# A two-layer tower on one core: turns of tiles moved between a layer's head, its attention loop and the feed-forward part of the layer before

## The chip, the core and the metric

The kernel runs on 1 core of one Trainium2 chip. Times are microseconds of the device. The time before is 2112.12 us, the median of 3 runs (2109.9 to 2117.12). Engines are called as the profile calls them: PE is TensorE's matrix multiply (PEld its weight load), DVE VectorE, ACT ScalarE, POOL GpSimd, SP the engine that issues the DMAs (SPq its queue).

## What is computed

8 x 256 tokens of width 192. First a token embedding with a layer norm, then four layers with banded attention (12 heads of 16; a token sees those within 64 positions), each with a feed-forward part of width 768; then an attention over channels, a feed-forward part with 4 experts, an unbanded attention, and one with 8 experts. The four layers in the reference:

```python
for l in range(L):
    q = heads(h @ Wq[l] + bq[l])
    k = heads(h @ Wk[l] + bk[l])
    v = heads(h @ Wv[l] + bv[l])
    a = band_attention(q, k, v, mask)
    a = a.transpose(0, 2, 1, 3).reshape(B, S, Hd)
    h = layer_norm(h + a @ Wo[l] + bo[l], ln1_s[l], ln1_b[l])
    f = jax.nn.gelu(h @ W1[l] + b1[l], approximate=False)
    h = layer_norm(h + f @ W2[l] + b2[l], ln2_s[l], ln2_b[l])
...
h = h + _L1_attn_ref(_layernorm(h, axis=-1), ...)      # softmax(q k^T * SCALE) v, 12 heads
```

## The kernel before

The 2048 tokens are 16 tiles of 128 (NT), in 4 groups of 4 (GT). Each engine's program is written out by hand in order; engines meet at semaphores, and an engine does nothing that stands behind a wait. A hardware loop (Fori) runs the four layers.

**Turning a tile.** To multiply h it must lie with its features on the partitions. TensorE transposes a tile in two halves into a PSUM bank (L364, in pe_transpose), ScalarE copies it, rounded, to xx (L569, act_split), and VectorE makes the two remainders from the same bank (L654, L655, dve_split). Turns use banks 0 and 1 by turns (BX), so the turn of tile t waits, through xx_ready, for the split of tile t - 2.

**A layer's head.** At its start TensorE turns tiles 0 to 3, then makes the projections of group 0 (items 0 to 6: three of q and k, L382 to L386, and four of v, L392 to L396) and the first three of group 1 (AHEAD), with the turns of tiles 4 to 15 between them (beside). q and k are cut into three bf16 pieces each: ScalarE copies the projection (L587, L589), VectorE makes the pieces of group 0 (L663 to L665, dve_pieces), GpSimd those of later groups (L894 to L897, pool_pieces) and those of v (L931 to L934, pool_v). SP writes the pieces to DRAM (L908) and reads them back by heads (L917) into qx and kx, once all three pieces of the group are there. ScalarE's third copy of group 1 (act_qk with n = 5) waits for the first pieces that GpSimd makes of group 1, since it writes the same qf buffer; it stands ahead of the first exponential in ScalarE's program. GpSimd makes v pieces first (pool_v of group 0, then pool_pieces of group 1).

**The attention loop** runs over 96 pairs of heads p (PAIRS; 12 pairs to one sequence of 256 tokens). At pair p TensorE does, in this order, the scores of p (L469 adds the mask, L472; allowed two pairs ahead of the exponentials), the values of p - 5 (L501 to L503), the transposes of the probabilities of p - 3 (L483), and at pairs 1, 4, 7, 10 one more projection of group 1 into bank 3 (BM[0]); later groups have theirs at every third pair. ScalarE does the exponentials (L604, numbers 2p and 2p + 1) and between them the copy of the turned probabilities of p - 3 (L615). VectorE does max of p (L682), the remainder lo of p - 4 (L688), then at the pair behind a v projection its copy to vf (L674), then a step of finishing a tile (L702 to L715).

**Behind the loop** the attention's output of a group is turned (turn k = 1, from xn), multiplied by Wo (L392 to L396), added (L753, residual, half 0), normed (statistics L762 and L766, GpSimd's scale L843 and L844, affine L796 to L805), and turned again (k = 2, from h). The feed-forward part is pe_hidden: 24 steps n (6 to a group) with the features of n (L382 to L386, into banks 2 and 3), ScalarE's Gelu (L643) and the second product of n - 2 (L562 x8, into banks 4 to 7; the first of a group waits until the residual, half 1, has read the group before). under() hangs turns ahead of steps: k = 2 of group g + 1 at step 6g + 2, k = 1 of group g + 2 at 6g + 3, and the product with Wo at 6g + 5. A step without a turn takes 2.45 us. On VectorE dve_tail gives the order; for g = 0 to 4 it does the first affine of group g + 1, residual and statistics (half 1) of g - 1, the turns' splits (2, g + 1), the second affine of g - 1, and then the turn, residual and statistics of g + 2. GpSimd's pool_tail follows with the scales and with hb, the next residual's summand (L850).

## Time and profile before

| | before |
|---|---|
| median of 3 runs | 2112.12 us (2109.9 to 2117.12) |
| the profiled execution | 2105.01 us, its span 2103.2 us |
| PE busy | 1575.0 us, 75% of the span |
| DVE busy | 1356.9 us, 65% |
| ACT busy | 1109.5 us, 53% |
| POOL busy | 717.1 us, 34% |
| granted TensorE clock, mean | 0.876 of full |
| chain that ended last | PE 48%, DVE 24%, issue 12%, ACT 6%, DMA 4%, POOL 3% |

The span goes by stages: a banded attention takes 156 us (93 to 249, then from 393 to 549 and so on), what lies between two of them some 144 us, of which the feed-forward steps are the larger part; the four layers end at about 1275 us, the unbanded attention's loop runs from 1617 to 1784. Shares over the whole span say little here, since each stage has another engine that is late; the views by stretch and by time say more. In them a line has its start in us from the span's start, how long it (or the run of equal ones, x4 and so on) took, and in brackets how long the engine had been idle and what ended that. The granted clock is a share of 2.4 GHz; its two levels are 1.2 and 2.4 GHz.

### The profile page before, as it was taken

To read this page: it belongs to the slowest core of one execution; us is meant where nothing else is said; L and a number is where in the kernel's file an instruction comes from. 1 tells how busy PE (TensorE), PEld (TensorE's weight loads), DVE (VectorE), ACT (ScalarE), POOL (GpSimd) and SP (SyncE) were. 2 spreads that over 40 slices of the span, in tenths; PEclk is the share of its full clock that TensorE was granted. 3 is DMA by queue.
4 is the path that set the end of the run, shared out by engine and by line. 5 is a ranking of instruction groups with operands and counts; after the bars stand their busy time and mean duration, and the time that the engine had idled before them with its cause. 6 is when DMAs were issued, how large, how long until landed. Compare 5 with 4: busy or idle time off the path is not lost.

```text
span 2103.2 us, 47757 instructions
## 1 busy us (share of the span) xinstructions
PE 1575.0 (75%) x14634; PEld 1320.4 (63%) x14634; DVE 1356.9 (65%) x3622; ACT 1109.5 (53%) x3351; POOL 717.1 (34%) x989
## 2 busy tenths in 40 slices
PE   0588777798787798786898783875945887649993
PEld 0477666576576676675676672754944666449993
DVE  4688865688765789665888655243436998544444
ACT  0499632698523799323898221323524997225651
POOL 5644123534122542133541231012544340025551
PEclk9999889899798899798999795877976999669996
DMA  5868000875000955003864000004746580137875
GB/s 133 167 111 101 16 1 2 152 96 83 1 1 25 155 80 72 1 2 52 136 96 49 1 1 12 1 21 143 239 126 91 83 100 2 40 120 239 242 233 167
DMA packets 191388, 178.63 MB, mean 85 GB/s; under 512 B 23056, under 2 KB 176208, under 8 KB 190992
## 3 DMA queue, kind: packets, MB, share of 16 engines
q1 hardware_dynamic: 183824, 158.19, 38.4%
q0 software_dynamic: 7296, 17.18, 2.5%
q8 instruction: 130, 2.13, 0.5%
q14 instruction: 138, 1.13, 0.2%
HBM read 132.96 MB, written 42.34 MB: 83 GB/s over the span
## 4 chain that ended last, share of the span: by engine, by line
PE 48%; DVE 24%; issue 12%; ACT 6%; DMA 4%; POOL 3%; SPq 1%; DVEq 1%; ACTq 0%; POOLq 0%
DVE ptl L688 7%; PE bank L1261 6%; PE bank L483 5%; PE bank L562 4%; ACT pth L615 3%; PE bank L501 2%; PE bank L364 2%; DVE neg_max L682 2%; ACT prob L604 2%; PE bank L1247 2%; PE bank L382 2%; DVE h L805 2%; DMA kx<-qk_rows 1%; PE bank L472 1%; PE bank L386 1%
## 5 line engine op out<-in xcount | busy, mean ns | idle before, releaser
L604 ACT ACTIVATE prob<-bank,neg_max 128x192 f32<-128x192 f32 (+1 forms) x960 | 417.1, 440 | 67.5 <-DVE neg_max L682 32.2
L688 DVE TENSOR_TENSOR ptl<-bank,pth 128x512 f16<-128x512 f32 x480 | 329.3, 686 | 34.7 <-ACT pth L615 26.6
L682 DVE TENSOR_REDUCE neg_max<-bank 128x2 f32<-128x384 f32 (+1 forms) x480 | 273.6, 570 | 92.9 <-PE bank L472 90.3
L483 PE MATMUL bank<-ident,prob 128*128 128x128 f32 x1920 | 310.0, 285 | 0.0
L615 ACT ACTIVATE pth<-bank 128x512 f16<-128x512 f32 x480 | 286.9, 598 | 6.4 <-PE bank L483 6.4
L569 ACT ACTIVATE xx<-bank 128x256 fp32r<-128x256 f32 x256 | 94.2, 384 | 365.8 <-PE bank L364 360.0
L501 PE MATMUL bank<-v,pth 128*128 128x32 bf16 x1920 | 199.4, 180 | 107.1 <-DVE ptl L688 94.0
L501 PEld LDWEIGHTS bank<-v,pth 128*128 128x128 f16 x1920 | 154.0, 96 | 197.6 <-DVE ptl L688 187.4
L483 PEld LDWEIGHTS bank<-ident,prob 128*128 128x128 f32 x1920 | 205.6, 143 | 0.2
L604 ACT ACTIVATION_READ_ACCUMULATOR prob<-bank,neg_max 128x1 f32 x960 | 202.6, 211 | 0.0
L503 PE MATMUL bank<-v,ptl 128*128 128x32 bf16 x1920 | 193.6, 176 | 0.0
L502 PE MATMUL bank<-v,pth 128*128 128x16 bf16 x1920 | 190.1, 169 | 0.0
L843 POOL TENSOR_SCALAR rstd<-mv 128x4 f32<-128x4 f32 x52 | 12.0, 231 | 491.0 <-DVE mv L766 485.0
L472 PE MATMUL bank<-kx,qx 96*128 96x192 bf16 (+1 forms) x960 | 169.9, 259 | 7.5 <-DMA kx<-qk_rows 5.3
L364 PE MATMUL bank<-ident,h 128*128 128x128 f32 x256 | 58.6, 352 | 141.2 <-DVE xx L655 88.7
L502 PEld LDWEIGHTS bank<-v,pth 128*128 128x128 f16 x1920 | 157.0, 97 | 0.2
L503 PEld LDWEIGHTS bank<-v,ptl 128*128 128x128 f16 x1920 | 154.7, 96 | 0.0
L643 ACT ACTIVATE fbuf<-bank,b 128x512 f32<-128x512 f32 x96 | 65.9, 687 | 164.7 <-PE bank L386 164.7
L364 PE MATMUL bank<-ident,xn 128*128 128x128 f32 x256 | 62.2, 372 | 117.5 <-DVE xx L655 63.1
L469 PE MATMUL bank<-mask,ident 128*128 128x384 bf16 x384 | 130.4, 340 | 23.6 <-DMA kx<-qk_rows 23.6
L562 PE MATMUL bank<-w,fbuf 128*128 128x192 f32 x768 | 143.0, 332 | 0.0
L562 PEld LDWEIGHTS bank<-w,fbuf 128*128 128x128 f32 x768 | 133.7, 195 | 8.3
(273 smaller groups left out, 4250.0 us busy)
## 6 DMA issues: line engine op xcount, KB each, us to landing
xn<-in_e_seg SPq DMA_DIRECT2D x34, 768.0 KB, 6.8
qx<-qk_rows SPq DMA_DIRECT2D x240, 96.0 KB, 5.0
kx<-qk_rows SPq DMA_DIRECT2D x240, 96.0 KB, 7.2
qk_rows<-fbuf SPq DMA_DIRECT2D x80, 192.0 KB, 2.8
w<-in_e_w SPq DMA_DIRECT2D x23, 576.0 KB, 4.6
qk_rows<-piece_c SPq DMA_DIRECT2D x40, 192.0 KB, 3.0
hb<-in_e_w SPq DMA_DIRECT2D x11, 576.0 KB, 4.3
y_rows<-mask SPq DMA_DIRECT2D x8, 768.0 KB, 8.7
```

The source lines that it names most:

```text
L364: last = nc.tensor.transpose(bank[BX[t % 2]][:, c * P:c * P + P], src[:, t, c * P:c * P + P], ident[:, :])
L469: nc.tensor.matmul(o, ident_bf, mask[:, 2 * b + qt, :].unsqueeze(1).to_broadcast([P, 2, D]), start=True, stop=False)
L472: last = nc.tensor.matmul(o[:, e, :], qx[0:ROWS, b % 3, hd + e, qt * P:qt * P + P], kx[0:ROWS, b % 3, hd + e, ks], start=not banded, stop= ...
L483: last = nc.tensor.transpose(bank[BT[p % 2]][:, (2 * e + c) * P:(2 * e + c) * P + P], prob[:, qt, hd % PROBS, c * P:c * P + P], ident[:, :])
L501: nc.tensor.matmul(o2, pth[:, p % 3, w], v[:, 0:32], start=(c == 0), stop=False)
L502: nc.tensor.matmul(o1, pth[:, p % 3, w], v[:, 32:48], start=False, stop=False)
L503: last = nc.tensor.matmul(o2, ptl[:, p % 2, w], v[:, 0:32], start=False, stop=(c == 1))
L562: last = nc.tensor.matmul(bank[BY[t]][:, 0:D], fbuf[:, (n - 2) % 4, t * P:t * P + P], w2[:, c, :], start=(c == 0), stop=(c == FC - 1))
L604: nc.scalar.activation(prob[:, qt, hd % PROBS, c0:c0 + n], scores_at(u // 2, n)[:, u % 2, :], ACT.Exp, bias=neg_max[:, tile_no % 3, hd:hd ...
L615: nc.scalar.activation(pth[:, p % 3, :], bank[BT[p % 2]][:, :], ACT.Copy).then_inc(hi_ready.sem, 1)
L682: nc.vector.tensor_reduce(neg_max[:, t % 3, hd:hd + 2], scores_at(p, D if banded else S), AX.X, ALU.max, negate=True).then_inc(max_ready.s ...
L688: nc.vector.tensor_tensor(ptl[:, p % 2, :], bank[BT[p % 2]][:, :], pth[:, p % 3, :], ALU.subtract)\
```

## The change

1. **Tiles 0 to 3 of the next layer** are turned in the feed-forward part, ahead of steps 20 and 21 (under, with first), and split by VectorE at the end of dve_tail's round g = 3, behind the second affine of group 2. For the first layer they are turned ahead of the loop.
2. **The last group's statistics, scale and affine** leave dve_tail. VectorE does them in the next layer's head: the statistics behind the third pieces, the affine behind the last v copy of group 0. GpSimd's scale and hb of that group stand at the start of the next round of the loop, the scale ahead of pool_v of group 0, hb behind it.
3. **Tiles 8 to 15** are no longer turned in the head, but in the attention loop, one each at pairs 2, 3, 5, 6, 8, 9, 11 and 12 (next_turn), in bank 3, behind that pair's other work. The turn of a tile waits for the split of the tile before, or for the copy of the v projection before; a projection at pairs 4, 7, 10 waits for the split of the tile before. The unbanded attention does the same.
4. **In dve_tail** the splits (2, g + 1) come directly behind the first affine, ahead of residual and statistics, and the splits (1, g + 2) ahead of the second affine.
5. **SP** reads the first sequence's q and k by fours of heads, as soon as each piece is written (12 reads for each of three), and TensorE's scores wait for each four.

The core of the diff:

```diff
-        def pe_transpose(pe, it, s, t, src, ready, turn, n):
+        def pe_transpose(pe, it, s, t, src, ready, turn, n, inside=False):
 
             pe.wait_ge(ready.sem, ready.at(turn, n))
-            pe.wait_ge(xx_ready.sem, xx_ready.at(it, s - 1))
+            pe.wait_ge(xx_ready.sem, xx_ready.at(it, s if inside else s - 1))
+            o = bank[BM[0] if inside else BX[t % 2]]
             for c in range(2):
             last.then_inc(xt_done.sem, 1)
...
-            steps = {2 + i: (lambda i=i: (tile(GT + 2 * i), tile(GT + 2 * i + 1))) for i in range((NT - GT) // 2)}
-            steps["xx"] = xx
+            steps = {2: lambda: (tile(GT), tile(GT + 1)), 3: lambda: (tile(GT + 2), tile(GT + 3))}
+            steps["xx"], steps["inside"] = xx, lambda t: tile(t, True)
             return steps
 
-        def under(turn, out=None):
+        def next_turn(p):
+
+            if 2 <= p < 2 + 12 and p % 3 != 1:
+                return 2 * GT + 2 * (p // 3) - (p % 3 == 0)
+            return None
+        def under(turn, first, out=None):
+            for i in range(2):
+                steps[FC * (NG - 1) + 2 + i] = lambda i=i: (first(2 * i), first(2 * i + 1))
             return steps
...
         def pe_scores(pe, it, p, banded):
             b, qt, hd = where(2 * p)
+            if b == 0 and hd % 4 == 0 and qt == 0:
+                pe.wait_ge(first_in[hd // 4].sem, first_in[hd // 4].at(it, 16 * 12))
+            elif b and p % (PAIRS // B) == 0:
...
         def pe_attention(pe, it, banded, w, before):
 
             for n in range(ITEMS + AHEAD):
+                if n == 1:
+                    pe.wait_ge(y_read.sem, y_read.at(it, 0))
                 if n == ITEMS:
                     pe.wait_ge(xx_ready.sem, xx_ready.at(*before["xx"](2 * GT)))
                 pe_qkv(pe, it, n // ITEMS, n % ITEMS, w)
                 if n in before:
                     before[n]()
-            pe.wait_ge(xx_ready.sem, xx_ready.at(*before["xx"](NT)))
                     pe_turn_probs(pe, it, p - 3)
                 if next_projection(p):
                     g, i = next_projection(p)
+                    if i == 0:
+                        pe.wait_ge(xx_ready.sem, xx_ready.at(*before["xx"](NT)))
+                    elif p and next_turn(p - 1):
+                        pe.wait_ge(xx_ready.sem, xx_ready.at(*before["xx"](next_turn(p - 1) + 1)))
                     pe_qkv(pe, it, g, i, w)
+                if next_turn(p):
+                    if next_projection(p - 1):
+                        g, i = next_projection(p - 1)
+                        pe.wait_ge(vf_ready.sem, vf_ready.at(it, 4 * g + i - 3 + 1))
+                    before["inside"](next_turn(p))
...
             act.wait_ge(xt_done.sem, xt_done.at(it, s + 1))
             nc.scalar.activation(xx[:, 0:2, t * P:t * P + P],
-                                 bank[BX[t % 2]][:, 0:2 * P].rearrange("p (a n) -> p a n", a=2),
+                                 bank[BM[0] if inside else BX[t % 2]][:, 0:2 * P].rearrange("p (a n) -> p a n", a=2),
...
+                if next_turn(p):
+                    split["inside"](next_turn(p))
...
                     dve_pieces(dve, ch, it, n)
                 elif n < ITEMS:
                     dve_v(dve, it, 0, n - 3, banded)
+                if n == 2 and banded:
+                    dve_last_stats(dve, ch, it)
                 if n in split:
                     split[n]()
+                if n == ITEMS - 1 and banded:
+                    dve_affine(dve, ch, it, 0, NG - 1, 1)
...
                     if i >= 3:
                         dve_v(dve, it, g, i - 3, banded)
+                if p and next_turn(p - 1):
+                    split["inside"](next_turn(p - 1))
...
+        def dve_last_stats(dve, ch, it):
+
+            dve_stats(dve, ch, it, 1, NG - 1, y_read, NT)
...
             def out(g):
-                dve_turn(dve, it, 1, g)
                 dve_residual(dve, ch, it, 0, g)
                 dve_stats(dve, ch, it, 0, g, o_read)
 
+            dve_turn(dve, it, 1, 0)
             out(0)
             dve_turn(dve, it, 1, 1)
             dve_affine(dve, ch, it, first(0), 0, 0)
-            dve_residual(dve, ch, it, 0, 1)
-            dve_stats(dve, ch, it, 0, 1, o_read)
+            out(1)
             dve_turn(dve, it, 2, 0)
             for g in range(NG + 1):
                 if g + 1 < NG:
                     dve_affine(dve, ch, it, first(g + 1), g + 1, 0)
+                    dve_turn(dve, it, 2, g + 1)
                 if g:
                     dve_residual(dve, ch, it, 1, g - 1)
+                if 1 <= g < NG:
                     dve_stats(dve, ch, it, 1, g - 1, y_read)
-                if g + 1 < NG:
-                    dve_turn(dve, it, 2, g + 1)
-                if g:
+                if g + 2 < NG:
+                    dve_turn(dve, it, 1, g + 2)
+                if 1 <= g < NG:
                     dve_affine(dve, ch, it, second(g - 1), g - 1, 1)
                 if g + 2 < NG:
                     out(g + 2)
+                if g == NG - 1:
+                    for t in range(GT):
+                        dve_split(dve, it + 1, t, t)
 
...
+                if g == 1:
+                    pool.wait_ge(first_out[i].sem, first_out[i].at(it, 32))
+                else:
+                    pool.wait_ge(pieces_out.sem, pieces_out.at(it, 96 * (g - 1)))
...
-            for i in range(3):
-                if g == 0:
+            def write(i, done):
...
-            sp.wait_ge(pieces_out.sem, pieces_out.at(it, 96 * (g + 1)))
...
+            if g == 0:
+                for i in range(4):
+                    if i < 3:
+                        sp.wait_ge(first_pieces.sem, first_pieces.at(it, i + 1))
+                        write(i, first_out[i])
+                    if i:
+                        sp.wait_ge(first_out[i - 1].sem, first_out[i - 1].at(it, 32))
+                        read(0, slice(4 * (i - 1), 4 * i), first_in[i - 1])
+                read(1, slice(0, HEADS), qk_in[1])
+            else:
+                for i in range(3):
+                    sp.wait_ge(next_pieces.sem, next_pieces.at(it, 3 * (g - 1) + i + 1))
+                    write(i, pieces_out)
+                sp.wait_ge(pieces_out.sem, pieces_out.at(it, 96 * g))
+                for b in (2 * g, 2 * g + 1):
+                    read(b, slice(0, HEADS), qk_in[b % 3])
...
-            for g in range(NG + 1):
-                if g < NG:
+            for g in range(NG):
+                if g < NG - 1:
                     pool_rstd(pool, ch, 0, g + 1 - NG, g, 1e-12)
...
             with pool.Fori(0, L) as it:
                 ch.enter(it, 160)
+                pool_rstd(pool, ch, it, 0, NG - 1, 1e-12)
                 pool_v(pool, ch, it, 0)
+                pool_hb(pool, it, normed(2, NT - GT) - 2 * NT, NG - 1, row_bo)
                 pool_pieces(pool, ch, it, 1)
                 pool_v(pool, ch, it, 1)
...
+            pool_rstd(pool, ch, L, 0, NG - 1, 1e-12)
+            pool_hb(pool, L, normed(2, NT - GT) - 2 * NT, NG - 1, row_bo)
...
+            for t in range(GT):
+                act_split(act, 0, t, t)
             with act.Fori(0, L) as it:
-                for t in range(GT):
-                    act_split(act, it, t, t)
-                act_attention(act, it, True, beside(lambda t: act_split(act, it, t, t)))
+                act_attention(act, it, True, beside(lambda t, inside=False: act_split(act, it, t, t, inside)))
...
-            for g in range(NG + 1):
-                if g < NG:
+            for g in range(NG):
+                if g < NG - 1:
                     dve_stats(dve, ch, 0, 0, g, None)
                 if g:
                     dve_affine(dve, ch, 0, g - NG, g - 1, 1)
+            for t in range(GT):
+                dve_split(dve, 0, t, t)
             with dve.Fori(0, L) as it:
                 ch.enter(it, 512)
-                for t in range(GT):
-                    dve_split(dve, it, t, t)
-                dve_attention(dve, ch, it, True, beside(lambda t: dve_split(dve, it, t, t)))
+                dve_attention(dve, ch, it, True, beside(lambda t, inside=False: dve_split(dve, it, t, t, inside)))
...
+            dve_last_stats(dve, ch, L)
+            dve_affine(dve, ch, L, 0, NG - 1, 1)
...
+            def first_turn(it, t, inside=False):
+                pe_transpose(pe, it, t, t, h, h_ready, it, normed(2, t) - 2 * NT, inside)
+
+            for t in range(GT):
+                first_turn(0, t)
                 pe.wait_ge(wa_ready.sem, wa_ready.at(it, 1))
                 pe.wait_ge(xx_ready.sem, xx_ready.at(it, GT))
-                pe_attention(pe, it, True, wa, beside(first_turn, lambda n: (it, n)))
...
                 pe_hidden(pe, it, wb, w2[0], tok_hidden,
                           under(lambda k, g: pe_turn(pe, it, k, g, 12 if (k, g) == (2, 2) else
                                                      16 if (k, g) == (2, 3) else None),
+                                lambda t: first_turn(it + 1, t),
                                 lambda g: pe_out_group(pe, it, wb, g)))
```

## Rows read from the trace of the kernel before

**Rows 1.** Stretches: length; PE, PEld, DVE, ACT, POOL busy us (instructions); granted clock, DMA share, GB/s.

```profile
93.00:249.00 156.00, 135.94 (x1918) 109.02 (x1916) 135.36 (x281) 138.10 (x504) 60.22 (x89) 0.97 0.62 94
249.00:272.00 23.00, 15.41 (x62) 11.60 (x60) 15.52 (x65) 4.51 (x12) 3.58 (x6) 0.50 0.00 1
```

**Rows 2.** TensorE in order of time, layer 0's last products: start, length, [idle before <-releaser].

```profile
351.72 4.06 PE L562 MATMUL bank<-w,fbuf 128*128 128x192 f32 x24
```

**Rows 3.** ScalarE in order of time: T, and exp 26.

```profile
392.85 0.78 ACT L587 ACTIVATE qf<-bank,bqk,q_scale 128x512 f32<-128x512 f32 x1 [5.39 <-POOL fbuf L897]
...
412.92 0.43 ACT L604 ACTIVATE prob<-bank,neg_max 128x192 f32<-128x192 f32 x1
```

**Rows 4.** GpSimd and the SP queue in order of time, feed-forward part and hand-over.

```profile
306.45 3.60 POOL L850 TENSOR_TENSOR hb<-h,row_bo 128x192 f32<-128x192 f32 x4 [2.65 <-DVE h L805]
...
358.95 1.04 POOL L844 TENSOR_TENSOR rstd<-rstd,neg_half 128x4 f32<-128x4 f32 x1 [0.18 <-POOL rstd L843]
378.40 0.34 POOL L931 CAST v<-vf 128x192 bf16<-128x192 f32 x1 [13.21 <-DVE vf L674]
...
388.75 0.61 POOL L894 CAST fbuf<-qf 128x512 bf16<-128x512 f32 x1 [0.33 <-POOL v L934]
...
380.40 2.75 SPq L917 DMA_DIRECT2D qx<-qk_rows  x6
```

**Rows 5.** VectorE in order of time, the hand-over.

```profile
355.81 1.15 DVE L753 TENSOR_TENSOR h<-bank,hb 128x192 f32<-128x192 f32 x4 [3.67 <-PE bank L562]
...
357.93 0.41 DVE L766 BATCH_NORM_AGGREGATE mv<-stats 128x2 f32<-128x6 f32 x4
...
371.51 0.69 DVE L663 TENSOR_TENSOR qf<-qf,fbuf 128x512 f32<-128x512 f32 x1 [4.07 <-ACT fbuf L589]
...
376.88 0.28 DVE L654 TENSOR_TENSOR xx<-bank,xx 128x128 fp32r<-128x128 f32 x1
```

**Rows 6.** TensorE in order of time, feed-forward parts of layers 0 and 1.

```profile
302.38 1.15 PE L364 MATMUL bank<-ident,h 128*128 128x128 f32 x4 [3.44 <-DVE xx L655]
...
306.87 0.60 PE L364 MATMUL bank<-ident,xn 128*128 128x128 f32 x4
...
343.07 0.53 PE L382 MATMUL bank<-xx,wb_hi 128*128 128x512 f32 x1
...
347.97 0.53 PE L382 MATMUL bank<-xx,wb_hi 128*128 128x512 f32 x1
...
626.40 0.60 PE L364 MATMUL bank<-ident,h 128*128 128x128 f32 x4
...
634.48 0.53 PE L382 MATMUL bank<-xx,wb_hi 128*128 128x512 f32 x1
```

**Rows 7.** VectorE in order of time, feed-forward part of layer 0.

```profile
301.78 0.29 DVE L654 TENSOR_TENSOR xx<-bank,xx 128x128 fp32r<-128x128 f32 x1
...
343.40 1.15 DVE L753 TENSOR_TENSOR h<-bank,hb 128x192 f32<-128x192 f32 x4 [10.34 <-PE bank L562]
...
351.45 0.69 DVE L805 SCALAR_TENSOR_TENSOR h<-hb,rstd,ln_b 128x128 f32<-128x128 f32 x1
```

**Rows 8.** TensorE and VectorE in the attention of layer 1, full clock.

```profile
397.69 0.41 PE L469 MATMUL bank<-mask,ident 128*128 128x384 bf16 x1
...
398.30 0.56 DVE L682 TENSOR_REDUCE neg_max<-bank 128x2 f32<-128x384 f32 x1 [0.57 <-PE bank L472]
399.11 0.69 DVE L688 TENSOR_TENSOR ptl<-bank,pth 128x512 f16<-128x512 f32 x1 [0.26 <-ACT pth L615]
```

**Rows 9.** The same engines just before, lower clock.

```profile
394.37 0.51 PE L392 MATMUL bank<-wa_hi,xx 128*128 128x192 f32 x1
...
395.54 0.54 PE L469 MATMUL bank<-mask,ident 128*128 128x384 bf16 x1
...
396.44 0.56 DVE L682 TENSOR_REDUCE neg_max<-bank 128x2 f32<-128x384 f32 x1 [1.18 <-PE bank L472]
```

**Rows 10.** The page's costliest groups: ScalarE's copy of a turned tile.

```profile
L569 ACT ACTIVATE xx<-bank 128x256 fp32r<-128x256 f32 x256 | 94.2, 384 | 365.8 <-PE bank L364 360.0
```

68 lines of the change are left out of this document (31 added, 37 removed).

## The prediction

> **What bounds the kernel now.** I read the stages first, then the hand-over between two layers, engine by engine. In the banded attention no engine has room: of 156.0 us ScalarE is busy 138.1, TensorE 135.9, VectorE 135.4 [rows 1]. So a wait put into that loop lengthens it, and work taken out of the gaps between stages shortens the kernel. The largest gap is the hand-over. TensorE ends a layer's feed-forward part at 355.78 (351.72 + 4.06) [rows 2], and the first softmax work follows the third copy of the next group's projections on ScalarE, L587, at 392.85; call that instant T. ScalarE's idle time before it, 5.39 us, was ended by GpSimd's L897, and exp number 26 (the first of pair 13) starts at 412.92, T + 20.07 [rows 3]. The hand-over is thus 37.1 us, and what ends last in it is a queue on GpSimd: v pieces from 378.40, q/k pieces of group 1 from 388.75 to T [rows 4]. The transfers of q and k land at about the same time. All times are those of the profiled execution (2105.0 us, span 2103.2); it is 7.1 us below the median of 2112.1, and I add every difference to the median.
>
> **Hand-over (three times, layers 0 to 1, 1 to 2, 2 to 3).** The last group's statistics and affine, the turns of tiles 0 to 3 and those of tiles 8 to 15 leave the path. The new path from the end of the feed-forward part: projection item 0 at the full clock 1.3 (half a plain step of 2.45 [rows 6] and its landing), two ScalarE copies of 0.78 [rows 3], three pieces on VectorE 5.4 (376.88 - 371.51), hence 8.3 [rows 5]. The residual L753 (1.15) holds item 1 for as long and is covered. Then dve_last_stats, 1.4 (from the residual's end, 356.96, to the aggregation's, 358.34) [rows 5]: 9.7. GpSimd now runs, ahead of pool_v, pool_rstd, which waits for these statistics: 1.65 to the end of L844 at 359.99 [rows 4], 11.4. pool_v takes 10.35 (378.40 to 388.75): 21.8. pool_hb of the last group, which used to run before, stands behind it: 3.6 (L850 x4): 25.4. The first q/k pieces 4.1: T at 29.6 instead of 37.1 [rows 3, 4]. **Saved: 7.5 each, 22.** VectorE's affine, under 5 long [rows 7], ends near 18 and is covered by pool_v. SP's earlier, smaller reads cost nothing as long as they land before T: written after 4.7 and 6.5, even with 36 reads issued 0.46 apart (six in 2.75 us before [rows 4]) the last lands near 32, and it is wanted by pair 4.
>
> **First layer and the unbanded attention.** In the prologue one affine and one set of statistics leave the path, about 5 (estimated from rows 5 and 7), while GpSimd gets pool_hb in its queue (3.6) and the wait for the scale (1.65): about +0.5. The unbanded attention has neither change: VectorE's first v copy stands behind the same pieces and splits as before, so GpSimd starts and ends as before: 0.
>
> **Feed-forward part (four times).** Two stalls go. At step 8 TensorE sits 3.44 us for VectorE's split of tile 8 and goes on at the lower clock; the step lasts 8.5, from 298.3 (302.38 less the gap and the first turns' 0.60) to 306.87 [rows 6]. VectorE splits at 301.78 only because residual and statistics come first [rows 7]. With the split at the end of the affine, 2.4 earlier (residual 1.15, statistics 1.4 [rows 5]), and the clock kept, the step is 5.1 long (two transposes' wait 1.6, features 1.3, values 1.2, and up to 1.0 since the second product now waits for the residual): 3.4 saved. Step 14 is its like: 634.48 - 626.40 = 8.08, to 4.8: 3.3 saved [rows 6]. One stall comes, and it is larger. The new turns of tiles 0 and 1 stand at step 20, of 2 and 3 at step 21; tile 2 needs bank 0 back, so TensorE waits for VectorE's split of tile 0. But VectorE's queue has, ahead of it, residual, statistics, the wait for GpSimd's scale and the whole affine of group 2: 343.40 to 352.1 [rows 7]. From the start of step 20 (343.07) tile 2 can go after 9.6, and step 21 then takes 4.5 cold (as from 302.38 to 306.87); before, both steps took 347.97 - 343.07 = 4.9 [rows 6]. Lost 9.2, of which some 6.7 are a gap. **Net +2.5, four times +10.** ScalarE's Gelu and everything else is queued behind TensorE there.
>
> **The loop (five times): the term that decides.** Tiles 8 to 15 are turned at pairs 2, 3, 5, 6, 8, 9, 11, 12, all through bank 3, which the projections of pairs 1, 4, 7, 10 use too. Each of these eleven pairs (2 to 12) now ends on TensorE with an item that waits for VectorE's last operation of the same pair, and the next pair's scores are queued behind that item. VectorE in turn takes max, lo and only then the split or v copy. So the engines go round in a ring: split to TensorE's start 0.6 (301.78 to 302.38) [rows 6, 7]; the turn of one tile 0.2 (at the lower clock two take 0.8 of the 1.15 at 302.38); scores to VectorE's max 0.61 (397.69 to 398.30); max 0.5, lo 0.6 (0.56 and 0.69 less what overlaps), then the next split [rows 8]. That is 2.5 a pair; with a projection (0.6) and a v copy in place of the turn and the split once in three pairs, these take about 7.65. Before, the 13 pairs up to exp 26 ran at 1.4 each [rows 3]. I start from T: projection, scores 2, v copy, turn and scores 3 bring the first split to T + 5.6, and eleven pairs on, exp 26 starts at T + 30.6: **+10.5 at the full clock.** At the lower clock a projection takes 1.17 (394.37 to 395.54), scores to max 0.90 (395.54 to 396.44), a turn 0.4: 3.0 a pair with a split and 9.5 for three; exp 26 at T + 36.5, **+16.4** [rows 9]. (Between T and the end of pair 1 TensorE has just been idle, so it starts low.) In the unbanded attention, with wider max and no mask product, the same ring gives +11 and +15.
>
> Which clock? TensorE's work, 135.9 / 96 = 1.4 us a pair, fills 56% of a ring pair of 2.5 us; at the lower clock, where a part of it doubles, about three quarters of one of 3.0 (an estimate). A stretch busy 15.41 of 23.00 us, 67%, was granted 0.50 throughout; the attention, busy 87%, 0.97 [rows 1]. So I take the lower level (1.2 GHz) for three quarters of the ring. The Trainium skill ("TensorE: Matmul & The Clock Gate", Part 1) says that the default state is throttled and that activity releases it; were two thirds busy enough for that, the ring would run at 2.4 GHz from early in each attention. The 23 us just named speak against it.
>
> **Sum.** Full clock: first layer 0.5, hand-overs -22, feed-forward +10, rings 4 x 10.5 + 11 = 53: +41. Lower clock: rings 4 x 16.4 + 15 = 81: +69. Three quarters of the way: +61, so 2166 for a profiled execution and **2173 by the median**. Removed work is nil: the same transposes, copies and splits are done, plus four tiles turned for a layer that doesn't come (in the last feed-forward part, under the stall).
>
> **Rivals.**
> A, the forecast: the ring at mostly the lower clock, 2160 to 2190. 0.5.
> B, the ring at the full clock, since the pairs' own transposes keep the grant up: 2112 + 41 = 2153. 0.25.
> C, no ring: the waits are met early, and a turn costs the loop only its ScalarE copy, 8 x 0.38 = 3.1 an attention [rows 10]: 0.5 - 22 + 10 + 15.5 = +4, 2116. Speaks for it: ScalarE is the busiest engine [rows 1]. Against: the order on TensorE and VectorE is fixed, and each link of the ring has its row. 0.1.
> D, faster: the turns ride in the loop's idle share (ScalarE idles 18 of 156 us [rows 1]) and cost nothing; what is left is 0.5 - 22 + 10 = -11.5, 2100. It decides as soon as an attention pays less than 2.3 us for its eight turns (11.5 / 5). Against: the same. 0.1.
> E, SP's 36 small reads land after T and hold pairs 2 and 4, or the delayed v pieces of group 1 hold pair 29: up to 5 us more an attention, 2190 to 2200. 0.05.
> That the layer's first tiles aren't turned early in effect is part of the sum: tiles 2 and 3 wait at step 21.
>
> **How the numbers follow.** A, B and E hold 0.8: the range is 2135 to 2195, its low end 18 below B for links that overlap more than their durations say, its high end in E. Faster by over 0.3% (6 us, about what a measurement of this kernel tells from none): 0.1, mainly D. Within: 0.1, C. Slower: 0.8.
>
> **What would show it.** Right: TensorE idle before L364 near the end of each feed-forward part for 6 to 7 us, released by VectorE's split; no 3.4 us gaps at steps 8 and 14; T 29 to 30 us after the feed-forward part's end, still released by GpSimd; in pairs 2 to 12 TensorE's idle time ended by VectorE's split, pairs 2.5 to 3.1 us apart, the granted clock near a half; exp 26 30 to 37 us after T. Wrong: if pairs stay at 1.4 to 1.7 us, the ring doesn't exist and C or D holds; if T comes below 25, GpSimd's queue isn't the bound of the new hand-over; if the gap at step 21 is missing, 37 us of the sum are gone.

## The result, and the profile of the changed kernel

The changed kernel takes **2181.1 us** (median of 4, 2178.6 to 2193.0) against 2111.0 for the kernel before (2104.7 to 2117.1): a ratio of 1.034, 95% interval 1.029 to 1.039. Its profiled execution took 2183.1 us, span 2181.1; that of before had a span of 2103.2. So 77.9 us have to be found. The prediction was 2173, range 2135 to 2195, slower.

The page of the changed kernel says where to look, though not yet why. First its busy times, then its group for VectorE's max (line, engine, operation, count | busy, mean ns | idle time before, and what ended most of it):

```profile
PE 1623.7 (74%) x14642; PEld 1354.6 (62%) x14642; DVE 1368.5 (63%) x3630; ACT 1115.8 (51%) x3356; POOL 707.7 (32%) x989
...
L707 DVE TENSOR_REDUCE neg_max<-bank 128x2 f32<-128x384 f32 (+1 forms) x480 | 273.6, 571 | 182.4 <-PE bank L485 180.2
```

And that group on the page of the kernel before:

```profile
L682 DVE TENSOR_REDUCE neg_max<-bank 128x2 f32<-128x384 f32 (+1 forms) x480 | 273.6, 570 | 92.9 <-PE bank L472 90.3
```

VectorE, ScalarE and GpSimd are about as busy as before; TensorE is busy 49 us more with eight more instructions, which fits the lower mean of its granted clock, 0.848 against 0.876. VectorE's idle time ahead of its max, ended by the scores, has doubled: 90 us more, with not a microsecond more work.

Then four landmarks in ScalarE's instructions divide every layer: the last Gelu, T, exp 26 and the last exp. In order of time, for the turn from layer 0 to layer 1, and T and exp 26 of layer 3:

```profile
379.90 0.69 ACT L668 ACTIVATE fbuf<-bank,b 128x512 f32<-128x512 f32 x1 [1.77 <-PE bank L389]
...
413.25 0.78 ACT L610 ACTIVATE qf<-bank,bqk,q_scale 128x512 f32<-128x512 f32 x1 [10.34 <-POOL fbuf L939]
...
450.90 0.42 ACT L627 ACTIVATE prob<-bank,neg_max 128x192 f32<-128x192 f32 x1 [0.85 <-DVE neg_max L707]
...
1047.85 0.78 ACT L610 ACTIVATE qf<-bank,bqk,q_scale 128x512 f32<-128x512 f32 x1 [10.21 <-POOL fbuf L939]
...
1079.31 0.42 ACT L627 ACTIVATE prob<-bank,neg_max 128x192 f32<-128x192 f32 x1 [0.54 <-DVE neg_max L707]
```

The same four instants in every kernel of this study, from its profiled execution (us; the five attentions are layers 0 to 3 and the unbanded one; each ratio is to the kernel before on the same chip, whose median was 2111.0 for the changed kernel, 2116.2 for e1 to e4, 2113.4 for e5 to e8, 2114.4 for e9 to e11):

| kernel | median | ratio, 95% | T to exp 26, five attentions | exp 26 to last exp | last exp to last Gelu, four layers | last Gelu to next T, three |
|---|---|---|---|---|---|---|
| before | 2111.0 | 1 | 20.0 20.1 20.4 20.4 20.9 | 130.6 132.0 131.0 132.0 129.3 | 109.0 110.7 110.4 110.4 | 40.9 40.8 41.1 |
| changed | 2181.1 | 1.034 (1.029-1.039) | 36.7 37.7 37.8 31.5 36.3 | 134.5 133.3 132.2 134.7 130.2 | 114.3 113.3 114.4 112.4 | 33.4 33.0 33.1 |
| e1 | 2101.9 | 0.994 (0.992-0.996) | 19.4 19.7 20.3 20.2 20.2 | 130.2 132.3 132.8 131.3 129.3 | 112.3 113.8 114.3 113.0 | 33.3 33.2 33.3 |
| e2 | 2165.5 | 1.024 (1.021-1.028) | 36.0 37.6 37.8 33.6 36.3 | 133.2 133.7 132.0 133.4 130.3 | 106.3 106.1 106.5 107.2 | 33.6 33.1 33.0 |
| e3 | 2130.4 | 1.006 (1.004-1.008) | 24.0 24.0 24.0 25.4 26.0 | 133.2 132.1 132.5 132.6 131.9 | 112.4 113.5 113.7 113.1 | 33.4 33.4 33.0 |
| e4 | 2087.4 | 0.987 (0.984-0.991) | 21.2 21.0 20.1 19.5 20.7 | 131.4 129.7 130.3 132.6 129.3 | 103.2 103.2 103.1 103.2 | 41.4 41.1 40.8 |
| e5 | 2178.4 | 1.031 (1.027-1.035) | 36.2 35.3 35.2 36.7 36.3 | 131.5 133.1 133.8 131.3 129.8 | 114.3 113.0 112.4 112.5 | 33.3 33.1 33.3 |
| e6 | 2071.8 | 0.981 (0.978-0.985) | 20.0 19.7 19.4 20.2 21.0 | 131.4 131.8 130.6 132.1 129.3 | 106.0 107.1 107.2 106.2 | 33.4 33.3 33.5 |
| e7 | 2091.1 | 0.990 (0.986-0.993) | 18.9 18.7 18.7 18.9 20.6 | 139.4 140.0 138.5 139.2 129.2 | 106.5 107.2 106.4 106.5 | 31.2 31.2 31.1 |
| e8 | 2066.5 | 0.979 (0.975-0.983) | 19.0 20.3 19.0 20.3 19.9 | 129.3 132.2 129.4 131.1 129.3 | 106.5 106.2 106.5 106.4 | 33.3 33.3 33.1 |
| e9 | 2065.8 | 0.979 (0.974-0.984) | 19.3 18.7 18.7 19.1 20.1 | 133.9 136.0 132.0 129.4 129.3 | 106.0 105.2 106.0 106.1 | 31.4 31.1 31.6 |
| e10 | 2054.3 | 0.974 (0.970-0.978) | 20.3 18.8 18.9 18.4 20.9 | 130.8 129.4 128.2 129.9 130.7 | 105.1 105.0 107.0 105.0 | 31.5 31.4 31.2 |
| e11 | 2142.5 | 1.014 (1.008-1.020) | 30.3 30.3 30.4 30.4 31.2 | 128.7 129.6 129.0 130.2 129.9 | 111.7 111.6 113.5 112.8 | 33.1 33.0 33.3 |

**Where the 77.9 us are**, by the first two rows before rounding: T to exp 26, 16.8 + 17.6 + 17.4 + 11.0 + 15.4 = **+78.2**; last exp to last Gelu **+14**; exp 26 to last exp **+9.9**; last Gelu to T **-23.4**; the first T +2.0 (it lies between 88 and 94 us in all profiled executions, so this one isn't explained by the change); the rest -2.7. The stretch from the last exp of the unbanded attention to the end, which no kernel here touches, took 334 to 345 us in these executions, so spans alone compare to a few us; the columns of the table do better.

**The pairs (answers to [rows 8, 9, 10]).** TensorE in order of time in pairs 1 to 7 of layer 1, only the instructions that waited, then four of layer 3:

```profile
414.08 0.53 PE L395 MATMUL bank<-wa_hi,xx 128*128 128x192 f32 x1 [10.23 <-ACT qf L610]
417.23 0.66 PE L367 MATMUL bank<-ident,h 128*128 128x128 f32 x2 [1.10 <-DVE vf L699]
419.63 0.69 PE L367 MATMUL bank<-ident,h 128*128 128x128 f32 x2 [0.25 <-DVE xx L680]
422.66 0.53 PE L395 MATMUL bank<-wa_hi,xx 128*128 128x192 f32 x1 [0.85 <-DVE xx L680]
426.40 0.66 PE L367 MATMUL bank<-ident,h 128*128 128x128 f32 x2 [0.44 <-DVE vf L699]
429.40 0.69 PE L367 MATMUL bank<-ident,h 128*128 128x128 f32 x2 [0.45 <-DVE xx L680]
432.43 0.53 PE L395 MATMUL bank<-wa_hi,xx 128*128 128x192 f32 x1 [0.44 <-DVE xx L680]
...
1057.12 0.36 PE L395 MATMUL bank<-wa_hi,xx 128*128 128x192 f32 x1 [1.26 <-DVE xx L680]
1059.96 0.41 PE L367 MATMUL bank<-ident,h 128*128 128x128 f32 x2 [0.92 <-DVE vf L699]
1062.40 0.44 PE L367 MATMUL bank<-ident,h 128*128 128x128 f32 x2 [0.92 <-DVE xx L680]
1064.87 0.36 PE L395 MATMUL bank<-wa_hi,xx 128*128 128x192 f32 x1 [0.92 <-DVE xx L680]
```

Every item through bank 3 waits for VectorE's last operation of the pair. Pairs with a turn are 3.00 apart in layer 1 (426.40 to 429.40) and three pairs 9.77 (422.66 to 432.43); in layer 3 they are 2.44 and 7.75. VectorE goes round with them, here in layer 1:

```profile
427.73 0.56 DVE L707 TENSOR_REDUCE neg_max<-bank 128x2 f32<-128x384 f32 x1 [1.57 <-PE bank L485]
428.21 0.68 DVE L713 TENSOR_TENSOR ptl<-bank,pth 128x512 f16<-128x512 f32 x1
428.81 0.28 DVE L679 TENSOR_TENSOR xx<-bank,xx 128x128 fp32r<-128x128 f32 x1
429.00 0.34 DVE L680 SCALAR_TENSOR_TENSOR xx<-xx,lo_rows,bank 128x128 fp32r<-128x128 f32 x1
430.76 0.56 DVE L707 TENSOR_REDUCE neg_max<-bank 128x2 f32<-128x384 f32 x1 [1.42 <-PE bank L485]
```

Split (429.34) lets the turn go at 429.40, the turn lets scores go, the scores the max at 430.76, then lo, then split. The two stretches from T to exp 26, of layers 1 and 3 (columns as in [rows 1]):

```profile
413.00:451.00 38.00, 31.17 (x223) 24.00 (x224) 17.17 (x43) 20.88 (x74) 16.81 (x28) 0.50 0.96 172
1048.00:1079.00 31.00, 20.35 (x222) 16.18 (x223) 16.77 (x42) 20.20 (x73) 15.23 (x26) 0.88 0.97 179
```

Nearly the same work, 223 and 222 TensorE instructions: at the lower level (1.2 GHz, granted 0.50) 38 us, at mostly the upper one (2.4 GHz) 31.

**The feed-forward part (answers to [rows 6, 7]).** TensorE at step 8 and at steps 20 and 21 of layer 0, then VectorE at step 21:

```profile
322.99 0.89 PE L367 MATMUL bank<-ident,h 128*128 128x128 f32 x4 [0.86 <-DVE xx L680]
...
361.22 0.60 PE L367 MATMUL bank<-ident,h 128*128 128x128 f32 x4
...
370.63 1.14 PE L367 MATMUL bank<-ident,h 128*128 128x128 f32 x4 [6.35 <-DVE xx L680]
```

```profile
361.42 1.15 DVE L784 TENSOR_TENSOR h<-bank,hb 128x192 f32<-128x192 f32 x4 [5.62 <-PE bank L585]
...
365.62 1.40 DVE L831 SCALAR_TENSOR_TENSOR hb<-h,mv,ln_s 128x192 f32<-128x192 f32 x4 [1.68 <-POOL rstd L883]
...
370.05 0.28 DVE L679 TENSOR_TENSOR xx<-bank,xx 128x128 fp32r<-128x128 f32 x1
```

The old gap of 3.44 us is 0.86. The new one is 6.35: tiles 0 and 1 are turned at 361.22, and VectorE splits tile 0 at 370.05, behind the residual and the affine of group 2.

**The hand-over (answers to [rows 4, 5]).** GpSimd in order of time; the feed-forward part's last products end at 383.76:

```profile
394.84 0.23 POOL L882 TENSOR_SCALAR rstd<-mv 128x4 f32<-128x4 f32 x1 [24.05 <-DVE mv L801]
...
396.25 0.34 POOL L986 CAST v<-vf 128x192 bf16<-128x192 f32 x1
...
407.00 2.22 POOL L889 TENSOR_TENSOR hb<-h,row_bo 128x192 f32<-128x192 f32 x4 [0.17 <-POOL v L989]
409.17 0.61 POOL L936 CAST fbuf<-qf 128x512 bf16<-128x512 f32 x1
```

T follows at 413.25, 29.5 us after that end, and the chain is the queue described in the prediction: scale, v pieces, sums, pieces.

### The profile page after: what moved, and what is told of

It reads as the page before. It is cut to its first block, busy times and chain, and to the rows that moved or that the text cites. A ratio compares the mean times of both kernels' runs of the same rounds, so it can differ in the third digit from the quotient of the medians.

```text
span 2181.1 us, 47962 instructions
## 1 busy us (share of the span) xinstructions
PE 1623.7 (74%) x14642; PEld 1354.6 (62%) x14642; DVE 1368.5 (63%) x3630; ACT 1115.8 (51%) x3356; POOL 707.7 (32%) x989
## 4 chain that ended last, share of the span: by engine, by line
PE 48%; DVE 25%; issue 13%; POOL 6%; ACT 5%; DMA 2%; DVEq 1%; SPq 1%; POOLq 0%; ACTq 0%
DVE ptl L713 7%; PE bank L1316 6%; PE bank L585 4%; PE bank L496 4%; PE bank L367 3%; PE bank L514 2%; PE bank L485 2%; ACT pth L638 2%; DVE neg_max L707 2%; DVE xx L680 2%; DVE h L840 2%; PE bank L1302 2%; PE bank L395 2%; PE bank L482 2%; PE bank L385 1%
## 5 line engine op out<-in xcount | busy, mean ns | idle before, releaser
L627 ACT ACTIVATE prob<-bank,neg_max 128x192 f32<-128x192 f32 (+1 forms) x960 | 416.3, 438 | 132.5 <-PE bank L496 69.6
L496 PE MATMUL bank<-ident,prob 128*128 128x128 f32 x1920 | 333.0, 300 | 0.0
L514 PEld LDWEIGHTS bank<-v,pth 128*128 128x128 f16 x1920 | 158.5, 98 | 177.2 <-DVE ptl L713 168.0
L496 PEld LDWEIGHTS bank<-ident,prob 128*128 128x128 f32 x1920 | 220.7, 151 | 0.2
L485 PE MATMUL bank<-kx,qx 96*128 96x192 bf16 (+1 forms) x960 | 177.2, 268 | 0.0
L367 PE MATMUL bank<-ident,h 128*128 128x128 f32 x264 | 65.3, 363 | 145.2 <-DVE xx L680 82.7
L515 PEld LDWEIGHTS bank<-v,pth 128*128 128x128 f16 x1920 | 159.9, 98 | 1.1
L367 PEld LDWEIGHTS bank<-ident,h 128*128 128x128 f32 x264 | 35.3, 174 | 172.1 <-DVE xx L680 88.2
L585 PEld LDWEIGHTS bank<-w,fbuf 128*128 128x128 f32 x768 | 132.5, 194 | 12.6 <-issue 5.2
```

The lines of the kernel that those rows point to most:

```text
L367: last = nc.tensor.transpose(o[:, c * P:c * P + P], src[:, t, c * P:c * P + P], ident[:, :])
L485: last = nc.tensor.matmul(o[:, e, :], qx[0:ROWS, b % 3, hd + e, qt * P:qt * P + P], kx[0:ROWS, b % 3, hd + e, ks], start=not banded, stop= ...
L496: last = nc.tensor.transpose(bank[BT[p % 2]][:, (2 * e + c) * P:(2 * e + c) * P + P], prob[:, qt, hd % PROBS, c * P:c * P + P], ident[:, :])
L514: nc.tensor.matmul(o2, pth[:, p % 3, w], v[:, 0:32], start=(c == 0), stop=False)
L515: nc.tensor.matmul(o1, pth[:, p % 3, w], v[:, 32:48], start=False, stop=False)
L585: last = nc.tensor.matmul(bank[BY[t]][:, 0:D], fbuf[:, (n - 2) % 4, t * P:t * P + P], w2[:, c, :], start=(c == 0), stop=(c == FC - 1))
```

## The experiments

The diffs are against the changed kernel where nothing else is said.

**e1: the turns of tiles 8 to 15 back in the head.** This separates the ring from everything else that the change does to the attention.

```
-            steps = {2: lambda: (tile(GT), tile(GT + 1)), 3: lambda: (tile(GT + 2), tile(GT + 3))}
+            steps = {n: (lambda i=i: (tile(GT + 2 * i), tile(GT + 2 * i + 1))) for i, n in enumerate((2, 3, 4, 5, 7, 8))}
...
-            if 2 <= p < 2 + 12 and p % 3 != 1:
-                return 2 * GT + 2 * (p // 3) - (p % 3 == 0)
             return None
...
+            pe.wait_ge(xx_ready.sem, xx_ready.at(*before["xx"](NT)))
             for p in range(PAIRS + 5):
```

> The changed kernel with tiles 8 to 15 turned in the head of the attention again (beside projection items 4, 5, 7 and 8) and none inside the pairs; all else of the change stays. Ring theory (each of pairs 2 to 12 goes once round TensorE, ScalarE and VectorE because its turn or projection waits for VectorE's last operation of the pair): exp 26 starts 20 to 21 us after T in every attention instead of 31.5 to 37.8, T itself moves by less than 4 us (there are about 10 us of slack before it, under GpSimd's v pieces), and the kernel takes 2181 - 78 + 0 to 10 = 2103 to 2113 us. Rival 1 (the pairs are slow because q and k arrive late through SP's smaller reads, or because GpSimd's v pieces now come later): exp 26 stays 30 us or more after T, 2165 or more. Rival 2 (the turns cost their work wherever they stand): T comes 10 us or more later and the kernel takes 2140 or more.

Measured: 2101.9 us, exp 26 at T + 19.4 to 20.3, and T where it was, 33.3 after the last Gelu. The ring theory holds and both rivals fall: the 78 us are due to the place of these turns, not to their work, nor to SP's reads, nor to GpSimd's later v pieces. In the head they cost nothing, since TensorE waits there for GpSimd in any case.

**e2: tiles 2 and 3 turned two steps later.**

```
-                steps[FC * (NG - 1) + 2 + i] = lambda i=i: (first(2 * i), first(2 * i + 1))
+                steps[FC * (NG - 1) + 2 + 3 * i] = lambda i=i: (first(2 * i), first(2 * i + 1))
```

> The changed kernel with the early turns of tiles 2 and 3 at step 23 of the feed-forward part instead of step 21; those of tiles 0 and 1 stay at step 20. Theory (tile 2 waits for its bank, held until VectorE splits tile 0 behind the residual, statistics and affine of group 2, which ends about 9 us after the turn of tile 0): the gap of 6.35 us at step 21 goes, the last Gelu comes 6 to 9 us sooner after the last exp in each of four layers, T stays 33 us after the last Gelu, and the kernel takes 2181 - 24 to 36 = 2145 to 2157 us. Rival (the stall only moves: VectorE's queue is late anyway and TensorE waits for the next thing from it, as the residual that frees the second product's banks): less than 2 us a layer, 2173 or more.

Measured: 2165.5 us, 15.6 less by the medians, 21 by the ratios; the theory had asked for 24 at least. Last exp to last Gelu fell by 5.2 to 8.0 us in the four layers, 28 in all, so the mechanism holds and each stall cost about 7 us. TensorE in order of time:

```profile
355.35 0.60 PE L367 MATMUL bank<-ident,h 128*128 128x128 f32 x4
...
364.78 0.89 PE L367 MATMUL bank<-ident,h 128*128 128x128 f32 x4 [1.45 <-DVE xx L680]
```

VectorE's queue is no later than before; TensorE simply has two steps of its own work to do meanwhile, and 1.45 us of the gap are left.

**e3: one turn in three pairs.**

```
-            if 2 <= p < 2 + 12 and p % 3 != 1:
-                return 2 * GT + 2 * (p // 3) - (p % 3 == 0)
+            if 3 <= p <= 24 and p % 3 == 0:
+                return 2 * GT + p // 3 - 1
...
-                    if next_projection(p - 1):
-                        g, i = next_projection(p - 1)
+                    if next_projection(p - 2):
+                        g, i = next_projection(p - 2)
```

> The changed kernel with the same eight turns inside the pairs, the same waits, but at every third pair (3, 6, ... 24) instead of two in three (2, 3, 5, 6, ... 12). Ring theory: what costs is that consecutive pairs are tied together, so a tie that ends after a pair lets the engines get ahead again; each turn then costs 0.5 to 1.2 us instead of about 2, the pairs up to 12 take T + 22 to 26 for exp 26, TensorE stays busy enough to be granted full clock there, and the kernel takes 2181 - 30 to 60 = 2120 to 2150 us. Rival (each turn through one bank costs a full round of about 2 us wherever it stands, neighbours or not): the time of the pairs up to 26 is the same as in the changed kernel and the kernel takes 2170 or more.

Measured: 2130.4 us, exp 26 at T + 24.0 to 26.0 (pairs 3 to 12 hold four of the eight turns), granted clock 0.87 from T to exp 26 in layer 1. From T to the last exp, against e1, the same eight turns with the same waits cost an attention 14.7 to 21.6 us in a row and 3.4 to 8.4 spread out. Part of that is the clock, but not most of it: in layer 3, granted 0.88 in a row and 0.79 spread out, it is 14.7 against 6.5. What costs is the unbroken chain of ties, not each tie. Against e1, where they stand in the head, they still cost 28 us of the kernel's time.

**e4: the kernel before with VectorE's new order alone.** Diff against the kernel before:

```
             def out(g):
-                dve_turn(dve, it, 1, g)
                 dve_residual(dve, ch, it, 0, g)
...
+            dve_turn(dve, it, 1, 0)
             out(0)
...
                     dve_affine(dve, ch, it, first(g + 1), g + 1, 0)
+                    dve_turn(dve, it, 2, g + 1)
                 if g:
                     dve_residual(dve, ch, it, 1, g - 1)
                     dve_stats(dve, ch, it, 1, g - 1, y_read)
-                if g + 1 < NG:
-                    dve_turn(dve, it, 2, g + 1)
+                if g + 2 < NG:
+                    dve_turn(dve, it, 1, g + 2)
```

> The kernel before with one part of the change alone: in the feed-forward part VectorE splits the turned tiles ahead of the residual and statistics of the group that has ended, instead of behind them. Theory of the prediction: steps 8 and 14 lose 3.4 and 3.3 us, the last Gelu comes 5 to 7 us sooner after the last exp in four layers: 2111 - 20 to 28 = 2083 to 2091 us. Rival (the residual, now later, holds back the second product's first matmuls by as much as the split used to hold back the first's): within 6 us of 2111.

Measured: 2087.4 us, ratio 0.987 (0.984 to 0.991); last exp to last Gelu shorter by 5.8 to 7.5 us. TensorE at step 14 of layer 0:

```profile
322.98 0.89 PE L364 MATMUL bank<-ident,h 128*128 128x128 f32 x4 [0.84 <-DVE xx L655]
...
325.29 1.54 PE L562 MATMUL bank<-w,fbuf 128*128 128x192 f32 x8 [0.25 <-DVE h L753]
```

The rival is visible, as a 0.25 us wait for the delayed residual. This part of the change is a plain gain of 24 to 29 us, hidden in the changed kernel by what the other parts cost.

**e5: the clock.** TensorE is kept busy in pair 1 before T.

```
+                if p == 1 and banded:
+                    for _ in range(50):
+                        nc.tensor.matmul(bank[BV[0]][:, 0:2 * D].rearrange("p (a n) -> p a n", a=2), ident_bf,
+                                         mask[:, 0, :].unsqueeze(1).to_broadcast([P, 2, D]), start=True, stop=True)
```

> The changed kernel with 50 idle products of 384 columns (the mask's product, into a bank that nobody reads before it is overwritten) on TensorE in pair 1 of each banded attention, in the 10 us in which it waits for the third projection copy. They add nothing to the result. Theory of the clock (the ring of pairs 2 to 12 lasts T + 37.5 where TensorE comes to it at the lower clock and T + 31.5 where it has been raised early, as in layer 3 of the changed kernel; the filler's 8 us at the full clock lie inside the wait): exp 26 starts 30.5 to 32 us after T in all four banded attentions, the granted clock of the 38 us after T is over 0.85, and the kernel takes 2181 - 18 to 24 = 2157 to 2163 us. Rival 1 (the ring's own busy share pulls the clock down again whatever came before): exp 26 stays at T + 36 to 38, 2178 to 2184. Rival 2 (the filler itself runs at the lower clock, 16 us, and delays T's successor): 2200 or more.

Measured: 2178.4 us, exp 26 at T + 35.2 to 36.7: rival 1, nearly. Stretches of layer 1 with T at 407.07:

```profile
404.00:405.50 1.50, 1.50 (x11) 0.88 (x9) 0.00 (x0) 0.00 (x0) 1.33 (x2) 1.00 0.25 69
...
411.50:413.00 1.50, 1.25 (x7) 0.75 (x6) 0.46 (x3) 1.14 (x4) 1.18 (x2) 0.50 1.24 125
...
414.50:416.00 1.50, 0.96 (x8) 0.89 (x9) 0.48 (x3) 1.19 (x5) 1.16 (x1) 1.00 1.40 147
...
419.00:420.50 1.50, 1.45 (x18) 1.04 (x15) 1.27 (x4) 0.53 (x3) 1.06 (x3) 0.50 0.97 392
```

The filler held the upper level until past T, and the clock fell in the first rounds of the ring, rose once, fell again and stayed. Coming to the ring with a warm TensorE isn't enough. Why layer 3 of the changed kernel kept the upper level with TensorE busy 20.35 of 31 us isn't settled by this run.

**e6: e1 and e2 together.**

> The edits of the first two experiments together: tiles 8 to 15 turned in the head, tiles 2 and 3 of the next layer at step 23. If the ring and the stall at step 21 are separate costs, their gains add: 2101.9 - (2181.1 - 2165.5) = 2086 us, last exp to last Gelu 106 to 107 us in each layer, exp 26 19.5 to 20.5 us after T, and T 33 us after the last Gelu. Rival (the head has no room once the feed-forward part ends earlier on VectorE's side): T 2 us or more later in each layer, 2092 or more.

Measured: 2071.8 us, ratio 0.981 (0.978 to 0.985), 14 below the forecast of plain addition. Against e1 each feed-forward part lost 6.3 to 7.1 us, as from the changed kernel to e2, and the median 30; it was the total of e2 that had shown too little (its stretch behind the last exp, which no edit touches, was 5 us longer than the changed kernel's). T didn't move. The two costs are separate.

**e7: GpSimd's four sums behind the next v pieces.** Diff against e6:

```
                 pool_v(pool, ch, it, 0)
-                pool_hb(pool, it, normed(2, NT - GT) - 2 * NT, NG - 1, row_bo)
                 pool_pieces(pool, ch, it, 1)
                 pool_v(pool, ch, it, 1)
+                pool_hb(pool, it, normed(2, NT - GT) - 2 * NT, NG - 1, row_bo)
```

> The kernel of the experiment with both edits, and GpSimd's four sums of the last group (2.2 us, which the change put between its v pieces and its q and k pieces) behind the v pieces of group 1. Theory (T is the end of GpSimd's queue: scale, v pieces, sums, first q/k pieces): T comes 2.0 to 2.4 us sooner after the last Gelu in three layers and in the first attention; exp 0 may follow it by up to 1.5 us, since q and k land about then, so each attention gains 1 to 2.2 us: 4 to 9 us below the kernel with both edits. Rival (T is bound by the arrival of q and k or by the q/k copies themselves): exp 0 doesn't move, 0 to 1 us in all.

Measured: T 2.1 us sooner and exp 26 at T + 18.8, so the theory of T is right; and yet 2091.1 us, 19 more than e6. Exp 26 to last exp grew by 7 to 8 us in each banded attention. TensorE at pair 24 (the first of the third sequence, exponential 48), and SP's queue, of e7, then SP's queue of e6, all of layer 1:

```profile
428.11 0.50 PE L480 MATMUL bank<-mask,ident 128*128 128x384 bf16 x1 [7.10 <-DMA kx<-qk_rows]
...
408.81 0.33 SPq L1507 DMA_DIRECT2D row_bo<-in_bo  x1
409.29 2.59 SPq L945 DMA_DIRECT2D qk_rows<-fbuf  x4
```

```profile
394.32 0.33 SPq L1507 DMA_DIRECT2D row_bo<-in_bo  x1
394.79 4.05 SPq L945 DMA_DIRECT2D qk_rows<-fbuf  x4
```

SP loads the next `row_bo` only when GpSimd's sums have read the old one (L1506 waits for them), and behind that load in SP's queue stand the writes of group 1's q and k pieces. They now start 22.2 us after T instead of 9.6, and TensorE pays 7.1 us of it.

**e8: the first batch read whole.** Diff against e6 (the scores of pair 0 wait for the one set of reads):

```
-            if b == 0 and hd % 4 == 0 and qt == 0:
-                pe.wait_ge(first_in[hd // 4].sem, first_in[hd // 4].at(it, 16 * 12))
+            if p == 0:
+                pe.wait_ge(first_in[0].sem, first_in[0].at(it, 16 * 12))
...
-                    if i:
-                        sp.wait_ge(first_out[i - 1].sem, first_out[i - 1].at(it, 32))
-                        read(0, slice(4 * (i - 1), 4 * i), first_in[i - 1])
+                for i in range(3):
+                    sp.wait_ge(first_out[i].sem, first_out[i].at(it, 32))
+                read(0, slice(0, HEADS), first_in[0])
```

> The kernel of the experiment with both edits, with SP reading q and k of the first batch as before, all twelve heads in 12 transfers after the third piece is written, instead of 36 transfers of four heads each as the pieces come. Theory of the prediction (the reads land before T either way, so the split in three is worth nothing): exp 0 at T + 0.7 to 1.5, the kernel within 4 us of the one with both edits. Rival 1 (smaller reads are what lets exp 0 follow T at 0.68 us instead of 1.3 to 2.8): 1 to 2 us a banded attention lost, 4 to 8 us slower. Rival 2 (36 issues of 0.46 us on SP delay batch 1 and the next writes): 3 us or more faster.

Measured: 2066.5 us, exp 0 at T + 0.68 with either. The split reads gain nothing. The median is 5.3 below e6's, outside the 4 us that were expected, but the ratios (0.979 and 0.981) can't be told apart. What changed for certain is SP's queue: its last read for the first two batches is issued at 377.0 (T - 3.9) instead of 390.0 (T + 4.8).

**e9: e7 with SP's load of `row_bo` behind the writes and reads of group 1.** Diff against e7:

```
-                sp.wait_ge(hb_ready.sem, hb_ready.at(it, 0))
-                sp.dma_start(row_bo[:, :], a["bo"][it + 1, :, :].to_broadcast([P, D])).then_inc(rows_bo.sem, 16)
                 for g in range(1, NG):
                     sp_heads(sp, it, g)
+                    if g == 1:
+                        sp.wait_ge(hb_ready.sem, hb_ready.at(it, 0))
+                        sp.dma_start(row_bo[:, :], a["bo"][it + 1, :, :].to_broadcast([P, D]))\
+                            .then_inc(rows_bo.sem, 16)
```

> The kernel with GpSimd's four sums behind the v pieces of group 1, and with SP's load of the next row_bo (which waits for those sums) also moved, behind the writes and reads of q and k of group 1, instead of ahead of them. Theory (what cost 8 us in every banded attention there, between exp 88 and exp 96, is SP's in-order queue: the load waited for the sums until 408.8 and the writes of group 1's pieces stood behind it, 14 us later than before, and TensorE waited 7.1 us for kx in pair 48): that gap goes, exp 26 to last exp is 131 us again, T stays 31.2 us after the last Gelu and exp 26 at T + 18.7, so four times 2.1 + 0.9 below the kernel with both edits: 2072 - 9 to 13 = 2059 to 2063 us. Rival (the sums delay GpSimd's weights and later pieces, which is what pair 48 waits for): 2085 or more.

Measured: 2065.8 us (2058.0 to 2070.9), 25 below e7 and 3 above the top of what was expected. SP's queue was the cause. (What the expectation calls pair 48 is exponential 48, of pair 24.) What is left of the wait, from the view of waits of layer 1's attention (us in total, times, longest):

```profile
PE bank L480 <- DMA kx<-qk_rows: 3.9, 1, 3.9
```

With T sooner, the 36 small reads end too late by as much. Layer 1 is the worst: in layers 0, 2 and 3 the wait is 1.7, 1.5 and 0.8 us.

**e10: e9 with e8's whole reads.**

> The kernel of the experiment just described, with the first batch's q and k also read whole, in 12 transfers. If both effects are independent (whole reads took 4 to 5 us off the kernel with both edits, by ending SP's reads of batches 0 and 1 some 6 to 9 us sooner), 4 to 5 us below it: 2054 to 2059 us. Rival (the gain of whole reads was the spread of the clock between profiled runs): within 2 us of it. With T 2 us earlier the reads of batch 0 are closer to the end: if exp 0 starts later than T + 0.7, 1 to 2 us a layer of it are lost.

Measured: **2054.3 us, ratio 0.974 (0.970 to 0.978)**, the fastest of the study and 2.6% below the kernel before. It is 11.5 below e9 by the medians, not 4 to 5. In e6 no attention waits for kx at pair 24, so whole reads had no such wait to remove; once T is 2 us sooner they remove that of layers 0 to 3, 7.9 us in all, and no attention of e10 waits there. So the two effects aren't independent, though e9's own runs lie 13 us apart and leave open by how much.

**e11: one link out of the ring.** VectorE's split ahead of lo.

```
+                if p and next_turn(p - 1):
+                    split["inside"](next_turn(p - 1))
                 if 0 <= p - 4 < PAIRS:
                     dve_lo(dve, it, p - 4)
...
-                if p and next_turn(p - 1):
-                    split["inside"](next_turn(p - 1))
```

> The changed kernel with VectorE's split of a tile turned inside the pairs ahead of its lo of that pair instead of behind it; nothing else moved. Ring theory (lo, 0.56 to 0.69 us, stands in the ring of each pair with a turn, so taking it off the chain shortens eight of eleven rounds by that much, and it has the TensorE part of the round to run in): exp 26 4 to 6 us sooner after T, T + 31.5 to 33.5 where it was 37.7, and 2181 - 18 to 28 = 2153 to 2163 us. Rival (TensorE's own work at the lower clock, 3.5 of every 4 us, is the bound of these pairs, and the ring's VectorE links are hidden behind it): exp 26 moves by less than 1.5 us, 2174 or more.

Measured: 2142.5 us (2131 to 2153), exp 26 at T + 30.3 to 30.4 in the banded attentions. The link, at the lower level in both kernels, from the turn of pair 3 to the projection of pair 4 of layer 1:

```profile
402.36 0.69 PE L367 MATMUL bank<-ident,h 128*128 128x128 f32 x2 [0.25 <-DVE xx L680]
404.79 0.53 PE L395 MATMUL bank<-wa_hi,xx 128*128 128x192 f32 x1 [0.25 <-DVE xx L680]
```

That is 2.43 us against 3.03 (419.63 to 422.66) in the changed kernel. But more than the link is gained: eight times lo is 5 us, and layers 0 to 2 gained 6.5 to 7.4. Its four stretches of 8 us from T on, layer 1:

```profile
395.97:403.97 8.00, 5.82 (x25) 4.39 (x26) 2.08 (x6) 5.35 (x20) 6.43 (x8) 0.50 1.18 125
403.97:411.97 8.00, 7.31 (x53) 5.58 (x52) 4.40 (x11) 4.62 (x17) 4.19 (x9) 0.50 1.00 274
411.97:419.97 8.00, 6.34 (x84) 5.12 (x82) 5.63 (x14) 5.59 (x21) 1.79 (x4) 0.94 0.61 200
419.97:427.97 8.00, 5.95 (x84) 4.85 (x85) 6.81 (x19) 6.09 (x23) 4.09 (x7) 1.00 1.17 124
```

The clock comes back some 17 us after T, after a stretch with TensorE busy 7.31 of 8.00 us, and stays. So e11 changed two things, the link and, by it or by chance, the clock. In layer 3, which the changed kernel ran mostly at the upper level, it gained 1.0. The rival, that cold TensorE work hides VectorE's links (less than 1.5 us), is refuted as it was put; but at the lower level TensorE idled only 0.44 to 0.45 us ahead of each item of pairs 5 to 7, so there a link of 0.6 is worth no more than that, and the rest goes with the clock.

## Why the prediction was right, and where it was off

It took 2173 for the median and 2181 came; for the profiled execution it took 2166 and 2183 came. (Its own terms give +62 where it wrote +61.) Term by term:

- **Ring: right in mechanism, size and places.** Rounds of 2.5 and 7.65 us were worked out for the full clock and 2.44 and 7.75 came; 3.0 and 9.5 for the lower, 3.00 and 9.77 came. Exp 26 was to start at T + 30.6 or T + 36.5; layer 3 ran at T + 31.5, layers 0 to 2 at T + 36.7 to 37.8. Three quarters of the way between the clocks made 74; 78.2 came, since four of five attentions ran the ring at or near the lower level (granted 0.55 in layer 0, 0.50 in the others). That share was taken from one row of before (67% busy, granted 0.50) and not worked out, and no run here explains it. e1 shows the cause, e11 a link.
- **Hand-over: right.** T 29.6 us after the feed-forward part's end, 29.5 measured; -22 for three, -23.4 measured. Two terms inside were off and happen to cancel: v pieces started 12.5 us after that end instead of 11.4 (TensorE's first product came 1.02 us late, after no wait that the profile shows, at the branch back to the loop's head), and the sums took 2.2 us instead of 3.6, because VectorE had the affine ready and GpSimd didn't wait between tiles. e7 shows that GpSimd's queue is what T hangs on.
- **Feed-forward part: right with one term too small.** Steps 8 and 14 gave 6.7 in the sum; e4 measured 5.8 to 7.5. The stall was put at a gap of 6.7, 6.35 measured, and at 9.2 in all; against e4 the changed part costs 10.4. e2 takes 7 of it away, so about 3.3 remain. By subtraction these are the four tiles' transposes and the waits that are left (1.45 us in e2); no run takes them out alone. The prediction had counted them as hidden under the stall. Net +10 was forecast, +14 measured.
- **What the sum lacked.** Exp 26 to last exp, +9.9, had no term. Some 8 of it lie right behind the ring, where VectorE forms the first finished tile (two products into xn) while GpSimd works on wb, the weights of the feed-forward part. Layer 1 of the changed kernel, then of before:

```profile
452.88 2.22 DVE L740 TENSOR_TENSOR xn<-au,rs 128x64 f32<-128x64 f32 x1
452.70 2.32 POOL L922 TENSOR_TENSOR wb_second_lo<-raw,wb_second 64x960 fp32r<-64x960 f32 x1
...
414.32 1.00 DVE L715 TENSOR_TENSOR xn<-au,rs 128x64 f32<-128x64 f32 x1
414.13 1.12 POOL L880 CAST wb_second<-raw 128x960 fp32r<-128x960 f32 x1
```

The same small product takes 1.00 us before, 2.22 in the changed kernel and 0.21 in e11, where it starts ahead of GpSimd's addition. In the first two it ends within 0.1 us of the GpSimd instruction beside it. The ring has moved it beside a longer one. (No run moves GpSimd's instruction alone; that the two hold each other up rests on these ends and durations.) From the max of pair 13 to that of pair 14 the four banded attentions take 4.72, 4.72, 4.72 and 5.84 us against 3.06 or 3.07 each, 7.7 in all, and the unbanded one 0.5 more; from that max to the last exp all five together take 645.8 against 644.8. With the ring gone (e1, e6) the step is back at 3.05 or 3.06, and in e11 it is 2.01 or 2.02. TensorE's clock, granted 0.88 in the 29 us after the ring of layer 1 against 1.00 in the same place of before, thus costs little there.
- **Rivals.** B came true in one attention of five. C fell: a turn is no mere ScalarE copy. D, faster, needed under 2.3 us an attention; e1, which takes the turns out of the pairs, lands where D said (2100 forecast, 2101.9 measured), but since it has no ring, not since the ring costs nothing. E named SP's small reads as a delay of pairs 2 and 4; they cost nothing there, but 0.8 to 3.9 us a banded attention at pair 24 once T is sooner (e9, e10).

The Trainium skill ("TensorE: Matmul & The Clock Gate", Part 1) has TensorE's activity release the throttle. e11 agrees: 7.31 of 8.00 us busy, then 1.00. The changed kernel's layer 1, busy 31.17 of 38 us and still at 0.50, shows that much activity doesn't always do.

## What to carry to other kernels

Work that is moved into idle time is free only if nothing on a second engine has to answer before the first goes on. If items in consecutive rounds share one buffer and each waits for the last operation of an in-order queue, the pipeline falls back to the sum of its latencies; space such items out, put the answering operation first in its queue, or do them in a stretch that waits for something else anyway. And of each operation that is moved, follow what its completion frees: here a small sum held a small load, and the load held the transfers of the next stage, for 19 us in all. Last, a delay of a stage moves what runs beside it: here the ring put a small VectorE product beside a longer GpSimd instruction, for 8 us in all that no term of the sum had.

## What the runs showed of the hardware

- Practically the same instructions (223 and 222) ran in 38 us at a granted clock of 0.50 and in 31 at 0.88. At the lower level the longer matmuls fill the ring (31.17 of 38 us busy), at the upper level they leave it a third idle (20.35 of 31). Layers 1 and 2 kept the lower level to the end of the ring, layer 3 the upper one once it had risen, 7 us after T; layer 0 and e5 reached the upper level early and lost it again. The clock before T doesn't decide it (e5).
- A VectorE product took 0.21, 1.00 or 2.22 us, by what GpSimd was doing beside it (the lines are shown above, at what the sum lacked).
- SP's issues cost by number, not by size: 36 reads of 32 KB were issued at about 2.8 us for six, and reads of 96 KB mostly in the same 2.8 us, some 0.46 us each (one six of each size took longer, 3.6 and 4.2 us).
